# Attention block kernel: q and k weights by groups of heads, short products in the score rings, last group's row sums on TensorE, last residuals in q's place

## What is computed

```
xn = layernorm(x)                                  # no scale, no shift
q, k, v = xn @ Wq.T + bq, xn @ Wk.T + bk, xn @ Wv.T + bv      # 16 heads of 32
scores = q @ k.T / sqrt(32), kept where (i % 256) >= (j % 256), else -1e30
s = softmax(scores) @ v, heads joined, @ Wo.T + bo
w = +1 where ffn_weights >= 0, else -1
g = silu(clip((xn @ w.T) * scale + bias, -100, 100))
out = x + s * g
```

## Time and profile before

| | us |
|---|---|
| median of three runs | 1934.47 (1933.18 to 1934.77) |
| profiled execution | 1935.96 |
| its span, first to last instruction | 1934.2 |
| PE busy | 1795.9 (93%) |
| DVE busy | 1448.5 (75%) |
| POOL busy | 1244.6 (64%) |
| ACT busy | 983.4 (51%) |
| mean granted TensorE clock | 0.982 |

### The profile page before, as it was taken

One profiled execution on the slowest core, in us unless ns is written; L12 is line 12 of the kernel. 1 busy time (PEld: TensorE's weight loads), 2 busy tenths in 40 slices (PEclk: granted clock), 3 DMA queues, 4 the chain that ended last, 5 costly groups with the idle time before them and its releaser, 6 DMA issues.

```text
span 1934.2 us, 34028 instructions
## 1 busy us (share of the span) xinstructions
PE 1795.9 (93%) x12104; PEld 779.6 (40%) x12104; DVE 1448.5 (75%) x2582; ACT 983.4 (51%) x1769; POOL 1244.6 (64%) x1080
## 2 busy tenths in 40 slices
PE   3889999999999999999999999999999999999877
PEld 2433444444444444444444344444444444444322
DVE  5687778677887778777687777877787776677754
ACT  3246555446554565545554465545555455544442
POOL 0046557875577757775668755787657775687676
PEclk8999999999999999999999999999999999999889
DMA  5401212222122211212211221222212221121102
GB/s 170 126 13 34 65 40 55 58 70 58 27 71 66 67 42 37 69 58 61 56 45 56 66 67 40 61 59 64 61 32 64 66 56 28 40 67 54 46 1 77
DMA packets 99258, 110.85 MB, mean 57 GB/s; under 512 B 23952, under 2 KB 73232, under 8 KB 98384
## 3 DMA queue, kind: packets, MB, share of 16 engines
q1 hardware_dynamic: 99088, 108.68, 20.5%
HBM read 41.23 MB, written 16.78 MB: 30 GB/s over the span
## 4 chain that ended last, share of the span: by engine, by line
PE 62%; DVE 16%; POOL 10%; issue 6%; ACT 3%; DMA 1%; SPq 1%; POOLq 0%; ACTq 0%; DVEq 0%
PE pJ L328 22%; PE pO L493 11%; POOL acc L816 8%; PE pS L449 8%; PE pT L473 7%; DVE mx L734 5%; PE pJ L433 3%; PE pJ L409 2%; PE pJ L410 2%; PE pJ L413 2%; PE pS L452 2%; DVE acc L766 2%; PE pT L469 2%; ACT PT L581 1%; DVE st L666 1%
## 5 line engine op out<-in xcount | busy, mean ns | idle before, releaser
L816 POOL TENSOR_TENSOR acc<-acc,PT 128x384 f32<-128x384 f32 (+1 forms) x756 | 890.0, 1200 | 500.8 <-PE pO L493 444.9
L734 DVE TENSOR_REDUCE mx<-pS 128x1 f32<-128x512 f32 (+3 forms) x1216 | 780.3, 655 | 314.8 <-PE pS L452 157.3
L581 ACT ACTIVATE PT<-pT 128x512 f32<-128x512 f32 (+1 forms) x960 | 540.3, 567 | 603.2 <-PE pT L473 543.8
L449 PE MATMUL pS<-QK 96*128 96x512 f16 (+3 forms) x1280 | 394.8, 320 | 33.9 <-DVE mx L734 32.6
L473 PE MATMUL pT<-QK 97*128 97x512 f16 (+3 forms) x1280 | 393.9, 318 | 6.8 <-ACT PT L581 5.7
L493 PE MATMUL pO<-PT,V 128*32 128x512 f32 (+3 forms) x2560 | 262.3, 482 | 8.6 <-ACT PT L581 8.1
L449 PEld LDWEIGHTS pS<-QK 96*128 96x128 f16 x1280 | 123.0, 97 | 317.8 <-DVE mx L734 136.2
L581 ACT ACTIVATE acc<-pT 128x512 f32<-128x512 f32 x256 | 151.0, 599 | 129.6 <-PE pT L473 129.2
L766 DVE TENSOR_TENSOR acc<-acc,PT 128x512 f32<-128x512 f32 (+1 forms) x204 | 173.3, 850 | 44.1 <-POOL acc L816 37.7
L469 PE MATMUL pT<-QK 128*128 128x128 f16 x1024 | 180.1, 220 | 10.7 <-ACT acc L581 8.0
L452 PE MATMUL pS<-QK 128*128 128x128 f16 x1024 | 181.8, 222 | 3.3 <-DVE mx L734 3.3
(11 more groups left out here) (96 smaller groups left out, 2607.7 us busy)
## 6 DMA issues: line engine op xcount, KB each, us to landing
QK<-sg SPq DMA_DIRECT2D x768, 64.0 KB
xr<-in_x SPq DMA_DIRECT2D x66, 256.0 KB, 3.0
out<-xr SPq DMA_DIRECT2D x64, 256.0 KB, 2.5
xs<-in_x SPq DMA_DIRECT2D x62, 256.0 KB, 3.2
QK<-aT SPq DMA_DIRECT2D x256, 1.0 KB, 1.7
acc<-in_wqT SPq DMA_DIRECT2D x1, 1024.0 KB, 8.0
acc<-in_wkT SPq DMA_DIRECT2D x1, 1024.0 KB, 12.2
QK<-in_mqk SPq DMA_DIRECT2D x2, 512.0 KB, 15.6
```

Source lines behind the costliest of these rows:

```text
L449: ins = e.matmul(pS[i % NPS][:, base:base + wide], q4[0:96, j, qc], k4[0:96, j, 0:wide], start=True, stop=True)
L581: e.activation(to, pT[i % 2][:, 0:cols], ACT.Exp, scale=SS).then_inc(s_p, 1)
L734: e.tensor_reduce(mx[:, par, part, :].rearrange("p (j q) -> p j q", q=4)[:, heads[0]:heads[-1] + 1, qi], pS[i % NPS][:, 0:cols].rearrange( ...
L816: e.tensor_tensor(a, a, PT[:, RING_AT[i] % NPT, 0:width * len(heads)].rearrange("p (j q) -> p j q", j=len(heads)), ALU.add).then_inc(s_ap, 1)
```

## The change

- **q and k weights by groups.** Wq and Wk are loaded in three parts each: the columns of group 0, of group 1, and of groups 2 and 3. The order is x 0 to 3, identity, q0, k0, biases, x 4 to 7, mask, V, mask, q1, k1, q2, k2. They are split in pieces of one group (128x512): q0, k0, the four pieces of V, then the six others from slot -34 on.
- **Start order.** x tiles 4 to 7 are planned at -74.1 to -71.5, among the first q and k; k of the second half ends at -61.7 and two V products follow. V products 3 to 7 of batch 0 move from -28.6 ... 23 to -26 ... 7.5. For group 0, ACT issues half of the placing DMAs (`place_first`).
- **Rings.** The x transposes take a turn in the ring of the three `pS` banks, the row sums of units 0 to 61 in the ring of the two `pT` banks. `pJ` keeps the products of 8 and more matmuls. The planned time of a row sum is 0.3 slots behind the first PV product of the next unit.
- **Last group.** Units 62 and 63 have no additions on POOL and DVE: PE multiplies each probability tile by ones and accumulates the row sums in a `pS` bank (`SUMMED`). ADD_P falls from 756 to 744 tiles, ADD_V from 204 to 186.
- **Last outputs.** The first four output projections of batch 7 move from 1205 ... 1223 to 1195 ... 1206; the last four are done for groups 0 to 2 ahead of time (two in `pJ`, two in `pS` banks) and finished with three matmuls each (`project_last`). The last 8 residual tiles are loaded to `QK[0]` in one go, results stay in the gate's tile, and DVE adds two of the last four.
- **Layer norm.** A Newton step has three small operations where it had four.
- Lengths and offsets of the plan are other numbers throughout.

```diff
+SUMMED = (NU - 2, NU - 1)
+def by_vector(n, kb):
+    return kb >= 4 * (n % NQS) + 2
...
+def at_sums(n):
+    return (at_pv(n + 1, 0) if n not in SUMMED else at_pv(n, 4 * (n % NQS) + 3)) + 0.01
...
     if kind == "x":
-        return (-84 if b < 4 else -64) + b if a == 0 else 4 * SL * a + (-80 + b if b < 4 else -65 + 0.9 * b)
+        return 4 * SL * a + (-82.58 + 1.71 * b if b < 4 else -66.0 + 2.4 * (b - 4))
...
+S_RING = sorted([(at_s(i), "s", i) for i in range(len(S_TILES))] +
+                [(wish("x", *divmod(i, NT)), "x", i) for i in range(B * NT)])
+T_RING = sorted([(at_t(i), "t", i) for i in range(len(T_TILES))] + [(at_sums(n), "sm", n) for n in range(NU - 2)])
+S_RING += [(0, "sm", NU - 2), (0, "sm", NU - 1), (0, "o", NTILE - 2), (0, "o", NTILE - 1)]
...
+        def rest(i):
+            k = i - NTILE + NT
+            return xr[i % 2][:, :] if k < 0 else QK[0][:, k // 4, k // 2 % 2, :, :].rearrange(
+                "p j t -> p (j t)").bitcast(F32)[:, k % 2 * D:(k % 2 + 1) * D]
+        def result(i):
+            return xr[i % 2][:, :] if i < NTILE - NT else gate(i)
...
-                        ln.wait_ge(*bank_free("x", b, t))
+                        ln.wait_ge(*s_bank_free("x", i))
...
+            def project_last():
+                b = B - 1
+                for t in range(NT // 2, NT):
+                    yield at("o", b, t)
...
+                    for g in range(NG - 1):
+                        n = (NG * b + g) % NSLOT
+                        e.matmul(out, Onh[:, n, ts], Wh["o"][:, g, :], start=False, stop=False)
+                        e.matmul(out, Onh[:, n, ts], Wl["o"][:, g, :], start=False, stop=False)
+                        e.matmul(out, Onl[:, n, ts], Wh["o"][:, g, :], start=False, stop=False)
+                yield past("sm", NU - 1) + 3.5
...
+                        if n in SUMMED:
+                            if kb == 0:
+                                ln.wait_ge(*s_bank_free("sm", n))
+                            for j in range(4):
...
+                                ins = e.matmul(sums_bank(n)[32 * j:32 * j + 32, 512 - width:512], ones[:, :], probs,
+                                               start=kb == 0, stop=kb == nkb - 1)
+                            ins.then_inc(s_last, 1)
...
+            def place_first():
+                for half in range(2):
+                    yield past("qk", 0, 2 * half + 1) + 1.99
...
+                        for j in range(2, 4):
+                            e.dma_start(QK[0][32 * r:32 * r + 32, :, half, j, :],
+                                        sg[32 * j:32 * j + 32, parts, cs]).then_inc(s_pl[half], 16)
...
-                        e.tensor_tensor(z, z, v, ALU.mult).then_inc(s_lv, 1)
-                        e.tensor_scalar(z, z, -0.5, 1.5, ALU.mult, ALU.add).then_inc(s_lv, 1)
-                        e.tensor_tensor(y, y, z, ALU.mult).then_inc(s_lv, 1)
+                        e.scalar_tensor_tensor(z, z, -0.5, v, ALU.mult, ALU.mult).then_inc(s_lv, 1)
+                        e.scalar_tensor_tensor(y, z, 1.5, y, ALU.add, ALU.mult).then_inc(s_lv, 1)
...
             def normalise():
-                    yield past("sm", n) + 0.5
+                    yield past("sm", n) + -0.16
...
+            def last_results():
+                for k, i in enumerate(LAST_V):
+                    yield past_o(i) + 1.2
+                    ln.wait_ge(s_t1, i + 1)
+                    ln.wait_ge(s_rest, 16 * NT)
+                    e.tensor_tensor(result(i), gate(i), rest(i), ALU.add).then_inc(s_fv, 1)
...
             def load_weights():
-                for key, when in (("q", -116), ("k", -115), ("v", -112), ("f", -40), ("o", -41)):
+                for name, when in (("q0", -117.5), ("k0", -117.4), ("v", -113), ("q1", -112.5), ("k1", -112.4),
+                                   ("q2", -111), ("k2", -110.9), ("o", -41), ("f", -40)):
...
+            def last_x():
+                yield at_t(T_FIRST[NU - 2, 0]) + 1
+                ln.wait_ge(s_T, T_FIRST[NU - 2, 0])
+                for i in range(NTILE - NT, NTILE):
+                    e.dma_start(rest(i), x_view[i // NT, i % NT]).then_inc(s_rest, 16)
```

More of the change, by code:

```diff
@@ L136 @@
     _now = max(_free, _todo[0][0])
-    _pick = next((x for x in _todo[:24] if x[0] <= _now + 0.01 and x[1][0] == "sm"), _todo[0])
-    _todo.remove(_pick)
-    PJ[_pick[1]] = max(_now, _pick[0])
+    _pick = _todo.pop(0)
+    PJ[_pick[1]] = _now
     PJ_INDEX[_pick[1]] = len(PJ_ORDER)
@@ L392, in project_o @@
                 for b in range(B):
-                    for t in range(NT):
+                    for t in range(NT if b < B - 1 else NT // 2):
                         yield at("o", b, t)
@@ L425, in row_sums @@
             def row_sums():
-                for n in range(NU):
+                for n in range(NU - 2):
                     yield at("sm", n)
@@ L504, in split_weights @@
             def split_weights():
-                for key in "qkvo":
-                    for h in range(4):
-                        yield {"q": -89, "k": -79.5, "v": -55, "o": 10}[key] + 0.5 * h
-                        ln.wait_ge(s_w[key], 16)
-                        e.activation(Wh[key][:, h, :], w_stage[key][:, h, :], ACT.Copy,
-                                     scale=SQ if key == "q" else SW).then_inc(s_wh, 1)
+                for n, (key, i) in enumerate(w_pieces):
+                    yield at_split(n)
+                    ln.wait_ge(w_load(key, i), 16)
+                    e.activation(w_part(Wh[key], key, i), w_part(w_stage[key], key, i), ACT.Copy,
+                                 scale=SQ if key == "q" else SW).then_inc(s_wh, 1)
             def layer_norm():
@@ L891, in place_qk @@
                         for r, parts in enumerate((slice(0, 3, 2), slice(1, 3), slice(0, 4, 3))):
-                            for j in range(4):
+                            for j in range(4 if gn > 0 else 2):
                                 e.dma_start(dst[32 * r:32 * r + 32, :, half, j, :],
@@ L906, in reload_x @@
             def reload_x():
-                for i in range(NTILE):
+                for i in range(NTILE - NT):
                     yield max(at("f", *divmod(i, NT)), past("o", *divmod(i - 2, NT)) + 3 if i > 1 else -99)
```

288 lines of the change are left out of this document (186 added, 102 removed).

## The result

| | before | after |
|---|---|---|
| median | 1934.22 us (1933.18 to 1934.77, 4 runs) | 1834.32 us (1833.56 to 1835.37, 4 runs) |
| ratio | | 0.9484, 95% interval 0.9468 to 0.9501 |
| span of the profiled execution | 1934.2 | 1832.9 |

The change takes 99.9 us off. Two of the three steps held in their sum, and the third, the steady part, is three and a half times the size given.

A forecast was written before the change was run, and what follows sets the result against it. PE was taken as the bound in the steady part, with waits at `pJ`. From 1935.96, minus 16 (start), 20 (steady part) and 13 (end) gave 1887, less 1.5 for the profiled execution about 1886; range 1863 to 1909.

The forecast's parts named there:

- Start, 16 gained: Start: first q product at 21.7 us, first S tile at 43 instead of 58.7; 16 us gained, bounds 8 and 20.
- Rival C: Start: DVE holds the S stage and first group, so only 8 of 16 us arrive; 1894 us, chance 0.08.
- End, 13 gained: End: last store 14.6 us earlier, less 1.5 for a later last T tile; 13 us gained.
- Steady part, 20 gained: Steady part: 31 us of `pJ` waits less 12 in the rings, 20 with the rest; bounds 36 gained, 29 lost.
- 31.2 us of waits at `pJ` go: Steady part, 200 to 1700 us: PE's waits at the two `pJ` banks, 31.2 us, disappear.
- Waits for maxima stay, the norm is worth 0: Steady part: 16.0 us of PE waits for maxima; 48 fewer norm operations on DVE gain nothing to 3 us, taken as 0.
- D: Steady part: DVE comes so late to the row sum that the T ring stands; slower than before, 1942 us, chance 0.04.
- First S tile: Sign for the start step: the first S tile starts at 43 us.
- New waits in the rings: Steady part: PE's waits at S tiles for maxima and at T tiles rise by about 12 us in all.
- PE idle 4 us less in each 300: Sign for the steady part: PE idles about 4 us less in each 300 us.
- A: Steady part: PE's waits move from `pJ` to `pT` and `pS`, gain falls to nothing; 1906 us, chance 0.20.
- B: End: PE fills 21 idle us and keeps the higher clock, last T tile 8 to 14 us earlier; 1874, chance 0.15.

The follow-up runs named there:

- e3: Kernel after with x transposes and row sums back in `pJ` and the steady part's places and offsets of before: 1904.21 us, ratio 0.9844 to before.
- e1: Kernel after with x transposes of batches 1 to 7 and row sums of units 0 to 61 back in `pJ`, new order kept: 1983.38 us, ratio 1.0247.
- e4: Kernel after with four small operations in a layer norm step instead of three: 1848.19 us, ratio 0.9554.
- e13: Kernel after with only the layer norm of batches 1 to 7 later, by 2.58 and 1.0 slots: 1880.95 us, ratio 0.972.
- e6b: Kernel after with the DVE, ACT and POOL offsets and the norm's times of before, rings and new places kept: 1887.12 us, ratio 0.9751.
- e2: Kernel after with the rings kept but all steady-part places and offsets of before: 1966.64 us, ratio 1.0168.
- e17: Kernel after with only q, k, V and output products at their old places and lengths: 1894.3 us, ratio 0.9794.
- e5b: Kernel after with the steady part's old places and lengths, rings and new offsets kept, norm moved along with the x tiles: 1963.3 us, ratio 1.0141.

## Why the prediction was wrong, step by step

**Start, 16 gained: right in size, short by the batch behind it.** The first q product was forecast for 21.7 and came at 19.92, S for 43 and came at 42.7. That S came so near is in part luck: the stretch between them took 22.8 us for my 21.1, and 1.9 of it is a wait of PE at 37.25 us for the `sg` of a q product, which ACT could take up only at 35.64, behind its placing DMAs. I had put ACT's blocking at nothing. DVE did not hold it: the S stage took 32 us to the first T tile where I allowed 36 (I put six splits into it, but those of group 1 run ahead of it, at 37.0 and 37.6 us on DVE, and are not planned from slot -34 on), and the first T tile is 15.4 us earlier. Then batch 0 gains too. In `e3`, which has the new start and the old rings and order, it takes 221.3 us for 227.0, 5.7 more, so the start as a whole gives some 20 (13.9 + 5.7 in `e3`). I had let the stage behind the S stage be shorter only by what the S stage was longer. Rival C (DVE holds the start) did not come.

**End, 13 gained: the tail right, the cost of its work too small.** Behind the last T tile, my times were 2.25 us to the end of the sums, 7.4 to the end of `Onl`, 11.7 to the last addition, 15.0 to the end of the span; they are 1.4, 6.6, 11.3 and 14.4. The tail gives 14.8 against 14.6. But I let the work ahead of the last T tile cost 1.5 us. In `e3` batch 7 takes 221.2 us for 215.6, 5.6 longer, and in the kernel after it gains 2.7 where the six before it gain 9.0 each. So it costs some 6, and the end gives 9. Start and end together: 29 forecast, 30.1 in `e3`, of which some 2 lie in batches 1 to 6, where the shorter norm is the main thing that is new. That the sum fits is luck: the start's error and the end's cancel.

**Steady part, 20 gained: the step that failed; about 70.** The difference of `e3` and after, 1904.2 - 1834.3, is 69.9 us. Three terms of the sum were wrong.

(1) "31.2 us of waits at `pJ` go": they did go, but the visible idle time is not their cost. From `e3` to after the matmuls in 200 to 1700 us rise from 9916 to 10307, which is 57 us of 1500, and PE's idle time falls by 33. The windows of `e3`:

```profile
200.00:1700.00 1500.00, 1447.28 (x9916) 634.47 (x9915) 1139.54 (x2033) 799.24 (x1442) 1021.29 (x889) 1.00 0.21 55
```

The rest, 23 us, is in the main wait time that lies inside the shown lengths of matmuls: 0.16 us or so of each visible wait, and all of the shorter ones; some 3 us of it are the granted clock. How much of the 57 is due to the `pJ` waits alone no run tells, since the rings alone lose. The means to see that waits cost more than they show stood in the trace of before, in the starts of two matmuls in a row. The share of PE in the chain that ended last is no such means, though it rose from 62% to 85%: before and `e3` have steady parts of nearly the same length and 62% and 72%, and `e1`, the slowest kernel of all, has 77%.

(2) "Waits for maxima stay, the norm is worth 0": they fell from 16.0 to 6.0, and the fourth operation alone costs 14 us (`e4`), the norm's place 46 (`e13`). I reasoned that PE waits for DVE only in a small part of the time. It does, but a norm operation that takes 0.9 us stands in front of a maximum, and the maxima are what PE waits for. I had cited the rule for this, of the Trainium skill (SBUF — State Buffer, "Who interferes with whom"), as something that could make the change slower. It worked for the change: the mean small operation went from 325 to 163 ns. With 57 operations fewer in the 1500 us that is 53 us of DVE's time. The trace agrees with the rule's instructions of two SBUF inputs and with its `copy`, which it lists among those that can take the shared ports. The row that I had cited it with, is an operation with one tensor as input, and so was no evidence for two.

(3) "Other numbers throughout" in the plan were costed only as far as they move DVE at the row sum. They carry the result: without them the rings lose 63 us. A step of the prediction should have asked what each of those numbers sets. The row sums' offset was seen right (D's price stands in `e6b`, 21.3 us of visible waits), the places of the long products, worth 60, not at all.

**The signs.** First S tile: held. No wait of the steady part at `pJ` on xTl, sg or R: held, but the x transposes still wait for xTl, now at `pS`. New waits in the rings: 12 forecast, 8.9 + 1.1 visible, so the size held, but not the place. They stand ahead of the x transposes; the waits of the S tiles for maxima and at `pT`, which were to rise, fell, from 16.0 and 2.3 us (L449 and L452) to 6.0 and from 4.4 to none. "PE idle 4 us less in each 300": it is 37.3 in 1500, 7.5 in each 300, nearly double. The last T tile was forecast for 1870 to 1875 and ended at 1818.5.

**Rivals.** A (waits move into the rings, 1906): no; it comes true in the old order (`e2`). B (the end gains more by its clock, 1874): granted clock in the last stretches, after:

```profile
1705.00:1765.00 60.00, 51.60 (x356) 20.19 (x354) 42.75 (x73) 29.69 (x55) 47.26 (x42) 0.91 0.10 23
1765.00:1816.00 51.00, 45.77 (x331) 17.07 (x330) 14.20 (x23) 24.52 (x45) 20.57 (x19) 0.97 0.19 63
1816.00:1833.00 17.00, 11.15 (x81) 5.03 (x78) 5.91 (x9) 2.42 (x4) 5.34 (x4) 0.91 0.17 62
```

It was 0.88 and 0.89. Over all of batch 7 and the tail the granted clock is 0.94 before (1689 to 1934 us) and 0.96 after (1605 to 1833), which is some 15 and 8 to 9 us off full speed. So the 6 us that the prediction left out of its sum did come; batch 7 got only 2.7 us shorter all the same, and the last T tile not 8 to 14 us earlier by it, as B has it. The prediction calls the 12.1 us "spent at 1.2 GHz"; with the lower level at half speed they are the loss, and the time spent there is twice that. D (slower): its mechanism is real with the old offsets, and is not in the kernel after. None of the rivals was the one that came: a steady part worth much more.

**Not settled.** Why the old places of the long products cost 60 us, the largest single price among the places, was not split further; the waits of `e17` are spread over four banks, none over 12 us. Whether the rings alone could pay at some other offsets was not tried.

## What to carry to other kernels

On engines that work in a fixed order, a change of banks and a change of the order are one change: price neither alone, and ask of every number of the plan what it sets. Where waits are short, count matmuls per window rather than idle time; every wait hides a part of itself in the shown length of a matmul. Small operations of DVE belong where GpSimd is quiet, and their worth is read from who stands behind them. Terms that are worth nothing in one order can cost a lot in another, so a zero in a sum needs its reason in the new order too.

## What was not expected of the hardware

A DVE operation on 128x4 elements takes 0.15 to 0.16 us alone and 0.77 to 0.93 beside running additions of POOL, a copy 1.00 us in the mean of 12 (`e5b`). That is about one POOL instruction (2.90 us for three, 0.97 each). A long stand of PE can cost more than its length. The same stretch of `e5b` in windows of 3 us (length, then busy times, then granted clock), around the stand of 2.77 us that ends at 674.14, and PE's first projection product behind it:

```profile
668.00:671.00 3.00, 3.00 (x27) 1.32 (x25) 2.93 (x8) 0.92 (x2) 1.77 (x2) 1.00 0.39 92
671.00:674.00 3.00, 0.37 (x6) 0.19 (x4) 2.93 (x5) 1.75 (x4) 3.00 (x4) 0.88 0.01 3
674.00:677.00 3.00, 2.86 (x17) 1.16 (x17) 3.00 (x6) 0.60 (x1) 0.51 (x1) 0.50 0.00 0
677.00:680.00 3.00, 3.00 (x21) 0.79 (x13) 2.23 (x6) 0.60 (x1) 0.00 (x0) 0.50 0.01 0
680.00:683.00 3.00, 3.00 (x21) 1.28 (x14) 1.38 (x2) 2.58 (x5) 0.00 (x0) 0.99 0.02 1
```
```profile
674.97 0.63 PE L421 MATMUL pJ<-wh_v,xTh 128*128 128x512 f16 x1
```

The clock was full up to the stand, is 0.50 (1.2 GHz) for the 6 us behind it, in which this form takes 0.63 us for 0.38, and is full again. So this stand costs its 2.77 us and, as an estimate from the half speed, some 3 more. Over 200 to 1700 us the granted clock is 0.98 in `e5b` and in `e1`, some 30 us of full speed, where before and after both have 1.00. That is a part of why the halves of the change lose as much as they do. In what the whole gains the clock has a small part in these 1500 us: before has 0.50 in 203.8 to 207.2, 432.5 to 435.9 and 889.9 to 893.3, some 5 us in sum, and after has none. The Trainium skill (TensorE: Matmul & The Clock Gate, "The HAM clock gate") has the rule that idleness takes the clock back; the trace agrees.
